# Moving the next group's feature and denominator stages into the feed-forward loop, and the broadcast copy from ScalarE to VectorE, in a transformer layer on 8 cores

## What is computed

```
n = layernorm(x)
Q, K, V = heads(n, Wq), heads(n, Wk), heads(n, Wv)        # 16 heads of 64
Qf, Kf = relu(Q/64**.25 @ P.T) + 1e-6, relu(K/64**.25 @ P.T) + 1e-6
KV = sum_n Kf V ; Ksum = sum_n Kf
out = (Qf @ KV) / (Qf . Ksum + 1e-6)
x = x + layernorm(out @ Wo.T + bo)
h = quantize(layernorm(x) @ w1 + b1)                      # 1024 -> 4096
h = piecewise_linear_gelu(h), quantized                   # 33 breakpoints
x = x + layernorm(quantize(h @ w2 + b2))
```

## Time and profile before

| what | value |
|---|---|
| time, median of 2 runs | 8509.85 us (8496.17 to 8523.53) |
| the profiled execution's own time | 8541.67 us |
| its span, slowest core (core 5) | 8539.7 us |
| spans of all cores | 8480.2 to 8539.7 us |
| median of die 0 and die 1 | 8491.8 us at a mean granted clock of 0.722; 8536.3 us at 0.692 |
| busy share of PE, DVE, ACT, POOL | 58%, 40%, 33%, 16% |

### The profile page before, as it was taken

How to read it: one execution, slowest core, us unless ns; L and a number is a source line. 1 busy time by engine, 2 the same in 40 slices (tenths; PEclk the granted TensorE clock), 3 DMA queues, 4 the chain that set the end, 5 groups by cost and what they waited for, 6 DMA issues and landing times.

```text
span 8539.7 us, 86539 instructions; the slowest of 8 cores (8480.2 to 8539.7 us)
## 1 busy us (share of the span) xinstructions
PE 4963.0 (58%) x24896; PEld 2705.6 (32%) x24896; DVE 3393.8 (40%) x6676; ACT 2798.1 (33%) x4257; POOL 1346.2 (16%) x1100
## 2 busy tenths in 40 slices
PE   0066556556667555555657656555566756666655
PEld 0033333333334333333323333333333433333332
DVE  1122444444432344444442244444443234444444
ACT  0021333333332233333332133333333223333333
POOL 0000111222210122221110011112221012222111
PEclk9976676766766666666666666666676666666676
DMA  4510111111120111111111011111112011111111
GB/s 144 177 55 30 50 50 54 50 50 50 52 77 16 57 52 52 52 52 53 52 50 56 30 50 50 55 50 50 50 52 77 15 55 54 53 52 52 54 51 47
DMA packets 124929, 475.64 MB, mean 56 GB/s; under 512 B 14614, under 2 KB 14871, under 8 KB 121387
## 3 DMA queue, kind: packets, MB, share of 16 engines
q1 hardware_dynamic: 114092, 419.78, 15.8%
q0 software_dynamic: 10368, 50.34, 1.6%
HBM read 419.72 MB, written 50.33 MB: 55 GB/s over the span
## 4 chain that ended last, share of the span: by engine, by line
DVE 32%; PE 26%; ACT 24%; issue 10%; DMA 5%; DVEq 2%; POOL 1%; ACTq 1%; SPq 0%; POOLq 0%
DVE poolF L912 6%; ACT poolF L230 4%; ACT poolF L902 3%; ACT poolF L907 3%; DVE poolF L916 3%; DVE poolF L920 3%; ACT poolF L924 2%; ACT poolF L928 2%; DVE poolF L217 2%; DVE poolF L793 2%; PE psT L261 2%; DMA poolF<-w_d 2%; DVE poolF L935 2%; PE psA L425 2%; PE psB L425 2%
## 5 line engine op out<-in xcount | busy, mean ns | idle before, releaser
L261 PE MATMUL psT<-idb,poolB 128*128 128x128 bf16 x1536 | 194.4, 307 | 1721.2 <-ACT poolB L763 578.0
L931 POOL TENSOR_TENSOR poolF<-poolF 128x512 f32<-128x512 f32 x512 | 649.7, 1269 | 2688.8 <-ACT poolF L928 2099.8
L912 DVE TENSOR_SCALAR poolF<-poolF 128x512 f32<-128x512 f32 x512 | 546.8, 1068 | 1235.6 <-ACT poolF L907 1235.6
L924 ACT ACTIVATE poolF<-poolF,cb 128x512 f32<-128x512 f32 x512 | 416.3, 813 | 1247.0 <-DVE poolF L920 1246.5
L261 PEld LDWEIGHTS psT<-idb,poolB 128*128 128x128 bf16 x1536 | 150.0, 139 | 1784.9 <-issue 1784.9
L939 POOL TENSOR_TENSOR poolF<-poolF 128x512 f32<-128x512 f32 x512 | 656.3, 1282 | 74.0 <-POOL poolF L931 0.9
L591 PE MATMUL psG<-lnf,wa 128*128 128x256 bf16 x2048 | 360.5, 336 | 495.4 <-ACT poolB L597 489.6
L813 PE MATMUL psA<-w2b,poolB 128*128 128x512 bf16 x1024 | 479.4, 468 | 173.6 <-DVE poolB L798 173.2
L891 PE MATMUL psF<-lnf,w1sb 128*128 128x256 bf16 x3584 | 519.6, 309 | 15.7 <-ACT poolF L907 15.7
L891 PE MATMUL psE<-lnf,w1sb 128*128 128x256 bf16 x3584 | 479.0, 293 | 0.6
L813 PE MATMUL psB<-w2b,poolB 128*128 128x512 bf16 x1024 | 478.8, 468 | 0.0
(11 more groups left out here) (166 smaller groups left out, 8155.2 us busy)
## 6 DMA issues: line engine op xcount, KB each, us to landing
w2b<-wsc SPq DMA_DIRECT2D x512, 512.0 KB, 3.6
yout<-poolF SPq DMA_DIRECT2D x64, 512.0 KB, 2.6
xbuf<-xin SPq DMA_DIRECT2D x48, 512.0 KB, 3.4
xbuf<-xin POOLq DMA_DIRECT2D x48, 512.0 KB, 4.9
poolF<-w_d SPq DMA_DIRECT2D x32, 512.0 KB, 3.6
poolF<-w_d SPq DMA_DIRECT2D x8, 2048.0 KB
wsc<-poolB SPq DMA_DIRECT2D x32, 256.0 KB, 2.3
x2b<-xin SPq DMA_DIRECT2D x16, 512.0 KB, 3.7
```

The source lines that it names most:

```text
L261: ttok = p.emit("T", lambda tt, src_slot=src_slot, dc=dc: tt.transpose(psT[:, dc * 128:(dc + 1) * 128], in_=poolB[:, src_slot + dc * 128:s ...
L912: xi4t = p.emit("V", lambda v, SL_A=SL_A, SL_B=SL_B: v.tensor_scalar(out=pf(SL_B, 512), in0=pf(SL_A, 512), scalar1=4.0, scalar2=4.0 * M1, ...
L924: y0t = p.emit("S", lambda s_, SL_E=SL_E, SL_D=SL_D: s_.activation(out=pf(SL_E, 512), in_=pf(SL_D, 512), func=AF.Gelu, scale=cb[:, CB_1:CB ...
L931: dtk = p.emit("G", lambda g_, SL_A=SL_A, SL_F=SL_F, SL_E=SL_E: g_.tensor_tensor(out=pf(SL_A, 512), in0=pf(SL_F, 512), in1=pf(SL_E, 512), ...
```

## The change

Four edits. The query stages go to one per iteration, it = 4 to 11. The feature stages go to two per iteration, it = 12 to 15, behind `emit_back` of their iteration; the denominator goes to it = 16, the reciprocal to 17. The spreading matmul becomes a stage of its own, `rex_stage` (L654 in the new file), and its first two are placed at it = 18 and 19. And in the attention output the copy of its result out of PSUM goes from ACT to DVE, with the matmul gH waiting for the product gH-2 (`a_ev`) where it waited for the copy gH-2 (`rex_ev`).

```diff
+                def rex_stage(gH, guard=()):
+                    bankR = psE if gH % 2 == 0 else psF
+                    st["rex_mt"][gH] = p.emit("T", lambda tt, bankR=bankR, gH=gH: tt.matmul(
+                        bankR[:, 0:256], lhsT=e16[:, gH * 128:(gH + 1) * 128],
+                        rhs=poolF[0:16, RD16:RD16 + 256], start=True, stop=True),
+                        waits=[st["rd_tok"]] + list(guard), inc=True)
...
                 for gH in range(8):
+                    if gH >= 2:
+                        rex_s(gH, [a_ev[gH - 2]])
...
-                    rex_ev[gH] = p.emit("S", lambda s_, bankR=bankR, rslot=rslot: s_.copy(
+                    rc = p.emit("V", lambda v, bankR=bankR, rslot=rslot: v.tensor_copy(
                         out=pf(rslot, 256), in_=bankR[:, 0:256]),
-                        waits=[mt, a_ev.get(gH - 2)], inc=True)
+                        waits=[att["rex_mt"][gH], a_ev.get(gH - 2)], inc=True)
...
-                    if it in (4, 6, 8, 10, 12, 14):
-                        att_stage_fns[0]((it - 4) // 2)
-                    elif it in (15, 16):
-                        att_stage_fns[0](it - 9)
-                    elif it in (17, 18):
-                        for gH in range(4 * (it - 17), 4 * (it - 16)):
-                            att_stage_fns[1](gH)
+                    if 4 <= it <= 11:
+                        att_stage_fns[0](it - 4)
+                    elif 12 <= it <= 15:
+                        att_stage_fns[1](2 * (it - 12))
+                        att_stage_fns[1](2 * (it - 12) + 1)
+                    elif it == 16:
+                        att_stage_fns[2]()
+                    elif it == 17:
+                        att_stage_fns[3]()
+                    elif it in (18, 19):
+                        att_stage_fns[4](it - 18, [h_ev.get(14), h_ev.get(15)])
```

More of the change, by code:

```diff
@@ L650, in rden_stage @@
                         waits=[rt], inc=True)
[L652 removed]
+                def rex_stage(gH, guard=()):
[4 more added lines that the diff above has]
+                        waits=[st["rd_tok"]] + list(guard), inc=True)
+                st["rex_mt"] = {}
+                st["rex_fn"] = rex_stage
+                return st, q_stage, qf_stage, den_stage, rden_stage, rex_stage
             att_pre = None
@@ L683, in build_program @@
                     rden_s()
+                    rex_s0(0, prev_h_ev)
+                    rex_s0(1, prev_h_ev)
                 qf_ev = att["qf_ev"]
@@ L689, in build_program @@
                     pending_final = None
-                rex_ev = {}
                 a_ev = {}
+                rex_s = att["rex_fn"]
                 for gH in range(8):
+                    if gH >= 2:
+                        rex_s(gH, [a_ev[gH - 2]])
                     bankR = psE if gH % 2 == 0 else psF
-                    mt = p.emit("T", lambda tt, bankR=bankR, gH=gH: tt.matmul(
-                        bankR[:, 0:256], lhsT=e16[:, gH * 128:(gH + 1) * 128],
-                        rhs=poolF[0:16, RD16:RD16 + 256], start=True, stop=True),
-                        waits=[rd_tok, rex_ev.get(gH - 2)]
-                        + (prev_h_ev if gH <= 1 else []), inc=True)
+                    bankA = psC if gH % 2 == 0 else psD
                     rslot = REX + (gH % 2) * 256
-                    rex_ev[gH] = p.emit("S", lambda s_, bankR=bankR, rslot=rslot: s_.copy(
+                    rc = p.emit("V", lambda v, bankR=bankR, rslot=rslot: v.tensor_copy(
                         out=pf(rslot, 256), in_=bankR[:, 0:256]),
-                        waits=[mt, a_ev.get(gH - 2)], inc=True)
-                    bankA = psC if gH % 2 == 0 else psD
+                        waits=[att["rex_mt"][gH], a_ev.get(gH - 2)], inc=True)
                     at = p.emit("T", lambda tt, bankA=bankA, gH=gH: tt.matmul(
@@ L714, in build_program @@
                         in0=bankA[:, 0:256], in1=pf(rslot, 256), op=ALU.mult),
-                        waits=[at, rex_ev[gH]], inc=True)
+                        waits=[at], inc=True)
                 ffn_guard = []
@@ L843, in build_program @@
                         px_next = emit_prologue_x(g8 + 1)
-                    if g8 + 1 < GB:
-                        if it == 3:
-                            pre_prologue = emit_prologue(g8 + 1, *px_next)
-                            att_n, q_s, qf_s, den_s, rden_s = make_att(
-                                pre_prologue[1], att["rd_tok"])
-                            att_stage_fns = (q_s, qf_s, den_s, rden_s)
-                        elif it == 19:
-                            att_stage_fns[2]()
-                            att_stage_fns[3]()
-                            att_pre = att_n
+                    if g8 + 1 < GB and it == 3:
+                        pre_prologue = emit_prologue(g8 + 1, *px_next)
+                        att_n, q_s, qf_s, den_s, rden_s, rex_s = make_att(
+                            pre_prologue[1], att["rd_tok"])
+                        att_stage_fns = (q_s, qf_s, den_s, rden_s, rex_s)
                     if it >= 4:
@@ L865, in build_program @@
                         att_late(it)
+                        if it == 19 and g8 + 1 < GB:
+                            att_pre = att_n
                         continue
```

5 lines of the change are left out of this document (2 added, 3 removed).

## The result

The changed kernel takes 8872.97 us (median of 11 runs, 8819.99 to 8924.17) against 8520.51 us for the kernel before beside it: ratio 1.0418, 95% interval 1.039 to 1.0446. It is slower by some 350 us, and 8872.97 lies in the forecast range of 8740 to 9130.

What follows compares the result with a forecast made beforehand. ACT, DVE and POOL set the loop's pace, PE works alone in the tail. Per group 18.5 - 7.0 + 1.6 + 1.5 = 14.6 us, over 28 groups 409, plus 2: 8921 us against the median; range 8740 to 9130.

Steps and rivals of the forecast that it cites:

- The main term: Loop iterations 12 to 15: feature stages take away PE's lead of a whole iteration, so the loop's end comes 18.5 us later.
- Three passages: The steps between iterations 12 to 13, 13 to 14 and 14 to 15, forecast to cost 18.5 us together.
- period 12.3: Forecast length of one step between iterations 12 and 15, 7.2 + 5.1 us, instead of 6.15.
- the half-clock spell: After PE's idling of some 5.5 us in each late iteration, PE was to run 4.7 us at half clock (1.2 GHz).
- T: End of DVE L798 in an iteration, from which the prediction counts; hidden matmuls were forecast done at T + 7.0.
- The tail: From iteration 15's end of DVE L798 to the bias step: 19.0 us forecast instead of 26.0, so 7.0 us saved.
- T_15: End of DVE L798 in iteration 15, where the loop's chains end and the stretch to the bias step starts.
- The output: Attention output: a DVE copy before each product, last product at 10.35 us instead of 8.7 from first to last, 1.6 us lost.
- The query stages: Iterations 4 to 11: PE's wait on ACT at iteration 5 and half clock after it, 1.5 us lost per group.
- PE's lead: Rival: second feature matmul's wait costs nothing, PE stays an iteration ahead, 11.8 us faster per group, 8180 us; chance 0.04.
- The short passages at a clock that never falls: Rival: clock holds up, every term at its low end, +4.8 us per group, 8644 us, within 2%; chance 0.08.
- The query stages' loop: Rival: 3 to 8 of its iterations 2.6 us too long at half clock, 9100 to 9460 us; chance 0.13.

## Why the prediction was right

**The main term** held in kind and nearly in size. Three passages cost 16.6 us where 18.5 were forecast. Its steps: the wait behind L611 (5.5 us of idling forecast, 6.06 and 5.77 shown), L921 at 0.43, `emit_po` at half clock, and period 12.3. The measured steps are 12.3, 12.1 and 11.7 on average, so the first passage, for which 12.95 was forecast, and the third were priced too high. The term that was mis-sized is the half-clock spell, 4.7 us taken from one row: in the first passage above the clock is up again 3.2 us after PE's restart (5191.62 to 5194.8), and over the 28 groups the spell is 4.0, 4.9 and 4.1 us on average in the three passages, between 2.9 and 6.3. The hidden matmuls are done 6.4 to 6.8 us after T on average, where 7.0 was forecast. Of the 1.9 us by which the term is off, 1.5 are the passages; the rest is the kernel before, whose last steps average 6.27 us over the groups and not the 6.15 of the two that I read.

**The tail** was forecast at -7.0 and is -7.25 on average, and that closeness is luck. The forecast was 19.0 us from T_15; the mean is 17.65. The kernel before was taken at 26.0, the value of one group; its mean is 24.90 (22.9 to 26.7). The two errors, 1.3 and 1.1 us, have the same sign and go out in the difference. In the group above, one of the longest, it is 20.1, with a wait of 0.99 us for the w2 transfer ahead of `emit_po(14)`, which I did not have, and the last bias matmuls at half clock. That T_15 starts it PE's wait shows, for the L611 behind it:

```profile
5227.13 0.37 PE L605 MATMUL psG<-poolB,pbd 128*128 128x256 bf16 x1 [5.77 <-DVE poolB L611]
```

**The output** was forecast at +1.6 and is +1.43. The products are 9.8 us apart from first to last, not 10.3 (8.7 before). The +1.43 is a net of two terms, of which I had one: the copy costs near 2 us by its two runs, and with the copy on ACT the stretch is 0.5 to 0.9 us shorter than the 74.53 of the kernel before. That gain goes with the two spreading matmuls that stand earlier; with them back behind the bias, in the kernel of the paired stages and the copy on ACT, it is 74.71.

**The query stages** were forecast at +1.5 and are +0.58: PE's wait at iteration 5 and the spell at half clock behind it are there (the step from 5 to 6 is 6.9 us), and the next step gets most of that back at 5.7 us. I had not counted on the slack being used to catch up.

Sum: +11.4 instead of +14.6 us per group. 8872.97 came out 48 us under the forecast of 8921; as a difference to the kernel before, 352 us where 411 were forecast. The mechanism of the main term and the signs of the others held.

**The rivals.** PE's lead did not survive. The short passages at a clock that never falls exist in every group only in the kernel with 80 unused transposes, and even they cost 10.3 us. The query stages' loop did not fall to half clock; the changed kernel has, in iterations 6 to 11 of the group above:

```profile
core 5: us, PE busy (x) PEld busy (x) DVE busy (x) ACT busy (x) POOL busy (x), PEclk, DMA share, GB/s
5150.00:5185.00 35.00, 30.67 (x183) 19.13 (x180) 21.51 (x36) 18.81 (x29) 12.92 (x11) 0.81 0.30 86
```

From iteration 6 to 12 the granted clock is 0.81 to 1.00 in each of the 28 groups, 0.96 on average, and at no moment half. In the kernel before the mean there is 0.86, with spells at half clock. So spreading the query stages evenly did to the clock the opposite of what this rival feared; the time shows little of it, since ACT, DVE and POOL set the pace of the loop.

The Trainium skill (TensorE: Matmul & The Clock Gate, "A second HAM failure mode: psum-queue depth-cycling") has short pauses between groups of matmuls as a cause of clock swings. With pauses of 0.75 us in each iteration of the query stages the steps stay at 6.17 to 6.21 us on average and the clock does not swing to half, so by this trace the rule costs nothing there.

## What to carry to other kernels

Where an engine runs an iteration ahead of the others, ask of every instruction that is put into its stream whether the answer that it waits for stands in the same iteration of the slower engine. If it does, all that stands behind it on the fast engine falls back by the whole chain, however short the instruction is, and 0.4 us of moved work costs 5.6; an answer of an iteration earlier cost nothing in the two kernels that had it. Such places show in a profile as single long steps in an even series, like the 13.7 us in the loop of the kernel before.
